# Rings of six for gathered rows and index lists in a graph network kernel, loops unrolled by six

## What is computed

```python
def _sage_conv(x, src, dst, ea, Wl, bl, Wr):        # three times
    msg = relu(x[src] + ea)
    agg = segment_sum(msg, dst) / maximum(cnt, 1.0)[:, None]
    return agg @ Wl + bl + x @ Wr
def _wgin_layer(x, src, dst, edge_weight, W1, W2):   # twice
    agg = segment_sum(edge_weight[:, None] * x[src], dst)
    return relu(agg @ W1.T) @ W2.T
def _gat_layer(x, src, dst, W, a_src, a_dst, b):     # three times
    h = (x @ W.T).reshape(N, 8, 8)
    e = leaky_relu(alpha_s[src] + alpha_d[dst])
    alpha = softmax of e over the edges of each dst
    return segment_sum(alpha[:, :, None] * h[src], dst).reshape(N, 64) + b
```

## Time and profile before

| | us |
|---|---|
| median of 3 runs, no profile | 17,362.4 |
| lowest and highest of them | 17,359.42 and 17,365.91 |
| span of the profiled execution | 22,236.9 |
| GpSimd (POOL) busy in it | 12,396.4 |
| TensorE (PE) busy in it | 10,574.4 |
| VectorE (DVE) busy in it | 6788.2 |
| ScalarE (ACT) busy in it | 3759.7 |

### The profile page before, as it was taken

The page is one execution under the profiler, slowest core; times in us unless marked ns, Lnnn a source line. Parts: engine busy times, 40 slices in busy tenths (PEclk is TensorE's granted clock), DMA queues, the critical chain, the costliest instruction groups (busy, mean ns, idle before and its releaser), DMA issues. The chain is left out here.

```text
span 22236.9 us, 220022 instructions
## 1 busy us (share of the span) xinstructions
PE 10574.4 (48%) x59536; PEld 9523.6 (43%) x59537; DVE 6788.2 (31%) x17499; ACT 3759.7 (17%) x5833; POOL 12396.4 (56%) x12932
## 2 busy tenths in 40 slices
PE   5777744444444421112111155555655555655555
PEld 5666634443444411111111145555455555455554
DVE  1111111111111111111111155555555555555555
ACT  0000000000000000000000033333333333333333
POOL 4555456665666646665666635555455555455553
PEclk5555555555555555555555555555555555555555
DMA  2222111111111111111111112222122222122221
GB/s 47 46 46 47 40 26 27 27 27 25 27 27 27 27 20 23 23 23 23 23 23 23 23 45 57 56 57 56 48 56 56 55 56 56 49 56 56 55 56 41
DMA packets 1022298, 881.00 MB, mean 40 GB/s; under 512 B 725873, under 2 KB 727665, under 8 KB 1022235
## 3 DMA queue, kind: packets, MB, share of 16 engines
q0 software_dynamic: 413696, 444.31, 11.0%
q1 hardware_dynamic: 608539, 435.96, 6.7%
HBM read 865.07 MB, written 14.17 MB: 40 GB/s over the span
## 5 line engine op out<-in xcount | busy, mean ns | idle before, releaser
L626 POOL DMA_INDIRECT rows<-node_table,idx x6464 | 6188.8, 957 | 3914.5 <-issue 1961.1
L1262 POOL DMA_INDIRECT rows<-gat_table,idx x4848 | 4680.8, 966 | 4606.8 <-DVE msg L1458 2707.4
L655 PE MATMUL bank<-sel,msg 128*64 128x48 f32 x10720 | 1292.5, 308 | 4484.4 <-DVE msg L691 1961.8
L655 PEld LDWEIGHTS bank<-sel,msg 128*64 128x64 f32 x10720 | 1194.0, 224 | 4582.8 <-DVE accT L668 1747.8
L1293 PE MATMUL bank<-avm,bufB 48*128 48x16 f32 x9696 | 2098.4, 363 | 630.3 <-ACT avm L1339 453.9
L1293 PEld LDWEIGHTS bank<-avm,bufB 48*128 48x128 f32 x9696 | 2033.6, 316 | 694.7 <-ACT avm L1339 469.5
L1417 DVE CUSTOM_DVE_ANT_0 far<-scores,far 128x1024 f32<-128x1024 f32 x1818 | 2129.3, 1221 | 487.4 <-remote 420.7
L626 POOL DMA_INDIRECT rows<-in_x,idx x1616 | 1526.6, 945 | 1162.9 <-issue 529.6
L1348 ACT ACTIVATE far<-bufA,subcol 128x1024 f32<-128x1024 int32 x1818 | 2063.4, 1147 | 508.1 <-issue 244.8
L655 PE MATMUL scores<-sel,msg 128*64 128x48 f32 x5440 | 655.9, 308 | 2272.9 <-DVE msg L691 968.1
L668 DVE TENSOR_TENSOR accT<-accT,bank 64x48 f32 x670 | 131.9, 197 | 5104.8 <-remote 3997.3
(11 more groups left out here) (150 smaller groups left out, 11092.9 us busy)
## 6 DMA issues: line engine op xcount, KB each, us to landing
bufA<-in_dst_rows SPq DMA_DIRECT2D x606, 512.0 KB
rows<-node_table,idx POOLq DMA_INDIRECT x6464
rows<-gat_table,idx POOLq DMA_INDIRECT x4848
bufA<-in_attr SPq DMA_DIRECT2D x202, 256.0 KB
bufB<-in_attr SPq DMA_DIRECT2D x606, 64.0 KB
idx<-in_src SPq DMA_DIRECT2D x1616, 4.0 KB
rows<-in_x,idx POOLq DMA_INDIRECT x1616
node_table<-tbuf SPq DMA_DIRECT2D x52, 128.0 KB
```

The lines of the kernel that those rows point to most:

```text
L626: nc.gpsimd.indirect_dma_start(rows[s][:, j, 0:D], None, table, bass.IndirectOffsetOnAxis(idx[s][:, j:j + 1], 0)).then_inc(s_rows[s].handl ...
L655: last = nc.tensor.matmul(bank[3 + s][0:D, 0:WIN], msg[s][:, j, 0:D], sel[s][:, j, :], start=j == 0, stop=j == G - 1)
L1262: nc.gpsimd.indirect_dma_start(rows[s][:, j, :], None, gat_table, bass.IndirectOffsetOnAxis(idx[s][:, j:j + 1], 0)).then_inc(s_rows[s].han ...
```

## The change

`RR = 6` is the ring of `idx` and `rows` in all passes. bufA, bufB, sel and msg have rings of R = 3 in all passes (in gat passes they had four), reached as `s % R`. All loops are unrolled by six: `turns` peels six groups, loops 33 - 1 = 32 times over six, and peels the last four. In gat passes SyncE also waits for `far_ready` of the group whose bufA is written over, with a semaphore increment between the two waits, and TensorE's `shifts` gets a semaphore increment. The number of groups, the edges in each and the windows stay as they are; the changes to constants such as `PARTS` write the same values in another form.

```diff
-RG = 4
+RR = 6
-        idx = [sb(f"idx{i}", [P, G], I32) for i in range(RG)]
-        rows = [sb(f"rows{i}", [P, G, ROW]) for i in range(RG)]
-        bufA = [sb(f"bufA{i}", [P, GE]) for i in range(RG)]
-        bufB = [sb(f"bufB{i}", [P, GE]) for i in range(RG)]
-        sel = [sb(f"sel{i}", [P, G, WIN]) for i in range(RG)]
-        msg = [sb(f"msg{i}", [P, G, ROW]) for i in range(RG)]
+        idx = [sb(f"idx{i}", [P, G], I32) for i in range(RR)]
+        rows = [sb(f"rows{i}", [P, G, ROW]) for i in range(RR)]
+        bufA = [sb(f"bufA{i}", [P, GE]) for i in range(R)]
+        bufB = [sb(f"bufB{i}", [P, GE]) for i in range(R)]
+        sel = [sb(f"sel{i}", [P, G, WIN]) for i in range(R)]
+        msg = [sb(f"msg{i}", [P, G, ROW]) for i in range(R)]
...
-        def turns(body, R=R):
-
-            for g in range(R):
+        def turns(body):
+
+            for g in range(RR):
                 body(g, g, 0)
 
             def rest(fori):
-                with fori(1, NG // R) as it:
-                    for s in range(R):
-                        body(it * R + s, s, it)
-                for g in range(R * (NG // R), NG):
-                    body(g, g % R, g // R)
+                with fori(1, NG // RR) as it:
+                    for s in range(RR):
+                        body(it * RR + s, s, it)
+                for g in range(RR * (NG // RR), NG):
+                    body(g, g % RR, g // RR)
             return rest
...
                         po.wait_ge(s_idx[s].handle, s_idx[s].at(it * 16 + 16))
-                        if due(g - R + 1):
-                            po.wait_ge(q["rows_free" if attr else "msg_ready"].handle, q["rows_free" if attr else "msg_ready"].at(g - R + 1))
+                        if due(g - RR + 1):
+                            po.wait_ge(q["rows_free" if attr else "msg_ready"].handle, q["rows_free" if attr else "msg_ready"].at(g - RR + 1))
...
-                        if due(g - RG + 1):
-                            sp.wait_ge(q["selT_ready"].handle, q["selT_ready"].at(g - RG + 1))
-                        sp.dma_start(bufA[s][:].bitcast(I32), A["dst_rows"][ds(g, 1), :].broadcast_to([P, GE])
-                                     ).then_inc(s_bA[s].handle, 16)
-                    turns(body, RG)(sp.Fori)
+                        if due(g - R + 1):
+                            sp.wait_ge(q["selT_ready"].handle, q["selT_ready"].at(g - R + 1))
+                            sp.sem_inc(s_passed.handle, 1)
+                            sp.wait_ge(q["far_ready"].handle, q["far_ready"].at(NSUB * (g - R + 1)))
+                        sp.dma_start(bufA[s % R][:].bitcast(I32), A["dst_rows"][ds(g, 1), :].broadcast_to([P, GE])
+                                     ).then_inc(s_bA[s % R].handle, 16)
+                    turns(body)(sp.Fori)
...
-                        if due(g - RG + 1):
-                            po.wait_ge(q["msg_ready"].handle, q["msg_ready"].at(g - RG + 1))
+                        if due(g - RR + 1):
+                            po.wait_ge(q["msg_ready"].handle, q["msg_ready"].at(g - RR + 1))
...
+                        pe.sem_inc(s_passed.handle, 1)
...
-                            if due(g - RG + 1):
-                                ve.wait_ge(q["sum_ready"].handle, q["sum_ready"].at(g - RG + 1))
+                            if due(g - R + 1):
+                                ve.wait_ge(q["sum_ready"].handle, q["sum_ready"].at(g - R + 1))
```

More of the change, by code:

```diff
@@ L197, in build @@
         s_passed = sem("waits_passed")
-        s_idx = [sem(f"idx_loaded{i}") for i in range(RG)]
-        s_bA = [sem(f"bufA_loaded{i}") for i in range(RG)]
+        s_idx = [sem(f"idx_loaded{i}") for i in range(RR)]
+        s_bA = [sem(f"bufA_loaded{i}") for i in range(R)]
         s_bB = [sem(f"bufB_loaded{i}") for i in range(R)]
@@ L231, in _ @@
                 ve.wait_ge(s_load.handle, s_load.at(16 * (len(loads) + 2)))
-                ends = st[0:HALF, 0:2, 0:2]
-                for h in range(2):
+                ends = st[0:PART, 0:2, 0:PARTS]
+                for h in range(PARTS):
                     src = group_dst[:, h * GE:(h + 1) * GE]
@@ L592, in sum_pass @@
         def sum_pass(name, table, attr=False, aux=False):
-            s_rows = [sem(f"{name}_rows_loaded{i}") for i in range(R)]
+            s_rows = [sem(f"{name}_rows_loaded{i}") for i in range(RR)]
             with nc.Block() as block:
@@ L647, in body @@
                             for j in range(G):
-                                last = nc.tensor.matmul(bank[6][:, 0:WIN], bufA[s][:, j * P:(j + 1) * P], sel[s][:, j, :],
+                                last = nc.tensor.matmul(bank[6][:, 0:WIN], bufA[s % R][:, j * P:(j + 1) * P], sel[s % R][:, j, :],
                                                         start=j == 0, stop=j == G - 1)
@@ L654, in body @@
                         for j in range(G):
-                            last = nc.tensor.matmul(bank[3 + s][0:D, 0:WIN], msg[s][:, j, 0:D], sel[s][:, j, :],
+                            last = nc.tensor.matmul(bank[3 + s % R][0:D, 0:WIN], msg[s % R][:, j, 0:D], sel[s % R][:, j, :],
                                                     start=j == 0, stop=j == G - 1)
@@ L1222, in gat_pass @@
         def gat_pass(name):
-            s_rows = [sem(f"{name}_rows_loaded{i}") for i in range(RG)]
+            s_rows = [sem(f"{name}_rows_loaded{i}") for i in range(RR)]
             edge = bank[4]
@@ L1264, in body @@
                                                          ).then_inc(s_rows[s].handle, 16)
-                    turns(body, RG)(po.Fori)
+                    turns(body)(po.Fori)
                 @block.tensor
@@ L1300, in sums @@
                         for j in range(G):
-                            last = nc.tensor.matmul(wide[s % 2][0:ROW, 0:WIN], msg[s][:, j, :], sel[s][:, j, :],
+                            last = nc.tensor.matmul(wide[s % 2][0:ROW, 0:WIN], msg[s % R][:, j, :], sel[s % R][:, j, :],
                                                     start=j == 0, stop=j == G - 1)
@@ L1450, in body @@
                         if real:
-                            ve.wait_ge(s_bA[s].handle, s_bA[s].at(it * 16 + 16))
-                            if due(g - RG + 1):
-                                ve.wait_ge(q["edge_ready"].handle, q["edge_ready"].at(g - RG + 1))
-                            nc.vector.tensor_scalar(bufB[s][0:WIN, :], bufA[s][0:WIN, :].bitcast(I32), first[0:WIN, ds(g, 1)], part[0:WIN, :],
+                            ve.wait_ge(s_bA[s % R].handle, s_bA[s % R].at(turn(s, it) * 16 + 16))
+                            if due(g - R + 1):
+                                ve.wait_ge(q["edge_ready"].handle, q["edge_ready"].at(g - R + 1))
+                            nc.vector.tensor_scalar(bufB[s % R][0:WIN, :], bufA[s % R][0:WIN, :].bitcast(I32), first[0:WIN, ds(g, 1)], part[0:WIN, :],
                                                     ALU.subtract, ALU.is_equal).then_inc(q["selT_ready"].handle, 1)
@@ L1486, in _ @@
                     n2 = link.close()
-                    for g in range(3, RG):
+                    for g in range(3, RR):
                         link.offset = n1 + n2 * (g - 2)
```

151 lines of the change are left out of this document (79 added, 72 removed).

## The result

The changed kernel takes 17,415.36 us (median of seven runs, 17,409.23 to 17,420.79) against 17,362.4 us before: ratio 1.003, 95% interval 1.002 to 1.004. It is 53 us slower, and that is beyond what the measurement leaves open. The time lies inside the range of 17,250 to 17,430 us, but past the 17,330 to 17,395 us of the forecast, on the side that had the chance of 0.07.

The account below looks back on a forecast made before the run. GpSimd's gather issue was taken to bound all eight passes, with no ring stall in timed runs. Every part was costed at 0: 17,362 + 0, given as 17,360 us; forecast 17,330 to 17,395 us, range 17,250 to 17,430 us.

Parts of the forecast that it names:

- The late ends as the cost of being recorded: TensorE matmul groups ending late in the trace, stalling VectorE then GpSimd (6595.6 us of waits in sum passes), blamed on profiling.
- the 4874.5 us: Profiled execution of 22,236.9 us less the unprofiled median of 17,362.4 us, taken as present only when the kernel is profiled.
- The bookkeeping of 16,378 + 1182: GpSimd's own gather work, 16,378 us, and windows between, before and after passes, 1182 us, set against the timed 17,362.4 us.
- Rings of six, worth 0: Deeper rings of gathered rows and index lists, all passes: gain 0 in timed runs, bounded above by 316 us.
- The slack of 15.3 us: Gat passes: index list behind bufA's wait was to land after 15.9 us and be wanted after 31.2 us; cost 0.
- Rings of three in place of four in the gat passes, 0: bufA, bufB, sel and msg wait for work one group younger; only bufA's wait moves, slack 8.8 or 7.5 us; cost 0.
- The added waits and increments, 0: Gat passes: far_ready always past when waited for; TensorE's increment under 0.1 us a group beside 1.3 us of slack; cost 0.
- Loops of six, 0: All passes: fewer branches, longer code; VectorE code loading hidden up to 7.7 us a turn; taken as 0.
- the second rival: Longer loops reload code each turn, in VectorE's gat loop: 17,583 us at an assumed 10 us a turn; chance 0.07 including late bufA loads.
- Stalls left (faster): Rival: ring stalls remain in timed runs, so deeper rings give 17,301 us, at most 17,046 us; chance 0.11.
- Ring not deeper in effect: Rival: in gat passes SyncE's order holds lists to four groups; 17,362 us, no change; counted within the forecast's 0.82.
- Code loading: Rival: VectorE's gat loop reloads code over 96 turns, 221 us at an assumed 10 us each; chance 0.07 including late bufA loads.

## Why the prediction was right or wrong

**What bounds the kernel.** Right where no end is late: in 12,920 steps inside passes of the kernel before GpSimd never stands longer than 0.3 us, and the gathers are 1.248 us apart in the sage passes and 1.270 in the gat passes (6154.1 us over 4845 steps).

```profile
POOL rows L626 <- issue: 2460.8, 8075, 0.3
POOL rows L1262 <- issue: 1376.2, 4516, 0.3
POOL rows L626 <- DMA idx<-in_src: 550.6, 5, 141.0
POOL rows L1262 <- DMA idx<-in_src: 408.5, 3, 178.1
POOL rows L1262 <- DVE msg L1458: 100.3, 329, 0.3
```

(8075 + 4516 + 329 = 12,920; the eight waits for lists are the starts of the passes.)

**The late ends as the cost of being recorded**. Wrong. The conclusion for the timed runs held because these were made on a chip without late ends, not for the reason given. The one rule that spoke against it, the Trainium skill, "Runtime: NRT & Kernel Launch", section "The launch sequence" (a profile's total stands a small fixed time above the executed time), was waved off with the 4874.5 us. The runs show a gap of 1.8 us (17,420.79 and 17,419.0) and 2.8 us (17,363.63 and 17,360.8), with the span, from the first to the last instruction, below the time and not above it: that the gap is small was right, and those 4874.5 us lay between two chips. Two numbers from two executions can't be subtracted before one kernel has been timed and profiled in the same place.

**The bookkeeping of 16,378 + 1182.** Both terms came from a trace with late ends. Where the time was measured they are 16,243 us in the passes and 1118 us around them: the gathers are busy for less (12,313.6 us for 12,396.4), and the idle time ahead of one is 0.304 us, not the 0.308 that the rounded 0.94 left. The conclusion, no stall, holds all the same.

**Rings of six, worth 0.** Right without late ends. With them it was wrong in sign for the step that moved the index list: in the sum passes that one stood behind bufB's wait and cost 2.0%, in the gat passes behind bufA's 1.7%. The slack of 15.3 us was reckoned for bodies that follow each other at the pace of the gathers. When a late end frees three groups at once, the slack is nothing. The prediction named the queue and then costed it for the smooth case alone.

**Rings of three in place of four in the gat passes, 0.** With late ends, rings of six and lists ahead, the gat passes took what they took before (8820 us). Not separated further.

**The added waits and increments, 0.** This is the first step that failed. "TensorE's is under 0.1 us beside 1.3 us of slack. Nothing." The size was right, 0.092 us. What was wrong is that slack swallows it. The delay goes by way of the factors and `z` to selT, and selT's place against a gather sets how long GpSimd is busy with that gather. Where it comes with gat loops and rings as they were, the gat passes are 25.0 and 29.2 us longer; how much of that is the increment's stays open.

**Work between passes.** The step that isn't in the prediction: it took that time as given, and no row of it was read for what a ring leaves behind. It was 15.5 us, 11.9 of them the drain of a ring of six at the end of five passes.

**Loops of six, 0.** Its bound looked at whether VectorE's body grows beyond the slack of 7.7 us a turn. The code is loaded again, as the second rival said, at 2.9 us a turn and in two of three gat passes, and that is hidden as computed. What was missed, here as with the increment, is that GpSimd's own step of 1.248 us isn't a constant: VectorE's timing, hidden or not, reaches it through the gathers that run beside selT. 40 us in the gat passes: 8.3 ns for each of 4848 gathers. Beyond the 25 to 29 us that are there without them, loops and rings of six have some 11 to 15 us of it in the profile of the change, and the runs don't part loop from ring. "Instruction fetch mechanics" in the same page of the Trainium skill (a taken branch to code outside the two pages held has to fetch it first) gave the event; the trace agrees in gat0 and gat1, not in gat2.

**What should be seen.** GpSimd busy 12,358 us, forecast 12,400; gathers 1.248 us apart: right. Late ends still there: only on chips that had them before. Gin passes shorter by 100 to 290 us, and a span of 21,600 to 22,100: neither. Where ends are late the gin passes took 4687.6 us after and 4698.9 before, and the span rose to 22,909.3. Recurring packets on the code queue were named as what would make it wrong, and were there.

**The rivals.** Stalls left (faster): excluded by the five lines above. Ring not deeper in effect: true in the gat passes, and it cost there. Code loading: it came, and hidden, so not at its price. The direction came from none of them: the 53 us are small terms, each costed at nothing.

## What to carry to other kernels

Before reading stalls, compare the profiled span with the time of the very run that was profiled; a gap to other runs may be another chip. A deeper ring is only as deep as the loads that feed it: put the small load ahead of the wait of the large one in the queue, and check the order for the burst, not for the steady pace. When one engine's issue bounds the kernel, look for what still reaches it: a deeper ring lengthened the closing drain here, and the issue step itself moved with what ran beside it, by a single added increment on an engine that had time to spare. And a kernel rebuilt with parts "as before" has to be compared line by line, or an addition that all variants share passes for no change at all.

## What the runs showed that I had not expected

- The same program at 17,362 to 17,375 us on some chips and 22,190 to 22,217 us on others (medians), no run of it in between. The granted clock was at the lower level (1.2 GHz) on both, 0.50 to 0.51 of full speed. On the second kind the wait "remote" for an end of TensorE reaches 33.9 us (40.0 with the change), and those followed in the timelines end 3.6 to 3.8 us after GpSimd begins its last gather before it stands at the ring (4029.07 to 4032.70, 4053.30 to 4056.86, 4027.38 to 4031.20). Why is open.
- GpSimd's drain at the end of a pass: it ends 4.9 to 5.1, 5.59, 7.6 to 7.9 and 8.9 to 9.2 us after the last gather begins, with two, three, four and six slots.
- A loop of some 305 recorded VectorE instructions loads five packets of 8 KB again each turn, or, in a copy at another address, none at all; one of 207 loads none.
- A gather is up to 0.3 us longer when VectorE's selT operation begins 0.3 us into it, and hardly longer when both begin together: in between it ends 0.12 us after selT does.
- One semaphore increment on TensorE delays the matmul behind it by 0.09 us, and in a kernel bound by GpSimd even that can be found again in the length of its gathers.
